# Second edge network: bias added by VectorE while it empties the bank, norm applied by ScalarE cell by cell

## The chip, the cores and the metric

One core of one Trainium2 chip. The metric is the device time of one execution in microseconds, the median of the runs shown; lower is better.

## The reference

Four graph layers in a row over 12500 nodes and 412500 edges. The change lies in the third, a mesh network whose edge state `e` (64 wide) goes through one network per step `s`, two steps:

```python
def _mlp(x, w0, b0, w1, b1):
    return jax.nn.silu(x @ w0 + b0) @ w1 + b1
def _ln(x, g, b):
    m = jnp.mean(x, axis=-1, keepdims=True)
    v = jnp.var(x, axis=-1, keepdims=True)
    return (x - m) * jax.lax.rsqrt(v + LN_EPS) * g + b
...
for s in range(S):
    ce = jnp.concatenate([e, n[senders], n[receivers]], axis=-1)
    e = e + _ln(_mlp(ce, edge_blk_w0[s], edge_blk_b0[s], edge_blk_w1[s], edge_blk_b1[s]), edge_blk_g[s], edge_blk_beta[s])
    agg = jax.ops.segment_sum(e.astype(jnp.float32), receivers, num_segments=num_nodes)
```

"Second edge network" is this line with s = 1. What the change touches is the output `... @ w1 + b1` and the factor `rsqrt(v + eps)` of its layer norm. The mean is taken out of the weights and of the bias ahead of time.

## The kernel before

The edges are sorted by target once and cut into 104 blocks. A block is 128 lanes by 35 cells (tile columns); a cell is 64 numbers on each lane. `sorted_mlp` (L1828) builds a pass over the blocks; it is called for both edge networks, with `rnd` 0 (`enc` true, which also encodes the edges) and `rnd` 1, which is the one in question. The names in the trace are the same for both; they are told apart by time. `PARTS5` (L1822) splits the 35 cells into five groups of 8, 8, 8, 8 and 3 cells, so 512 columns or 192; the last group's matmuls are padded to 256.

For a group of block k of the second network, in order:

- VectorE `picks` (L2079, L2080): three one-hot tables and one of the targets; `windows` (L2145 to L2151) splits the block's window of node rows into three bf16 parts, once a block.
- TensorE `gather` (L2474, L2481, L2486) takes the node terms into a bank `ps_h1`, `hidden1` (L2503) adds the edge state that SP loaded (`states`), with the spilled row (L2496) in the last group.
- ScalarE `act1_` (L2336): silu into `act1`.
- TensorE `out1` (L2506): a matmul of one row of biases into the bank (L2511, `row_eblk`), then eight of the weights (L2514), into one of two banks `ps_o1`.
- ScalarE `out1_` (L2338): copies the bank to `unit1` (L2344), then squares `unit1` into `sq1` (L2348).
- VectorE `var1` (L2139) sums the squares of each cell into `stat`; after all five groups `roots` (L2190 and `newton`, L555 to L569) turns these into scales, once a block.
- VectorE `norm1` (L2094) multiplies a group of `unit1` by its scales.
- The result is split into three bf16 parts for the sum by target: ScalarE `part0` (L2362), VectorE `less0` (L2107), ScalarE `part1` (L2366), VectorE `part2` (L2111). TensorE `part_sums` (L2526, L2528, L2530) adds them up in `ps_sum`, and VectorE `merge` (L2168 to L2180) finishes the block.

Every engine has its order written out by hand, three blocks deep: at turn k TensorE, ScalarE and VectorE work on block k-1 in the network (`main`) and on block k-2 behind the root (`out_`), VectorE also makes the first two groups' picks of block k and merges block k-3. `in_pairs` (L88) writes out six turns and then loops over pairs. There is one `unit1`, so a group of it can be filled only when `less0` of that group of the block before has read it.

VectorE's turn before the change (`body`, L2207; M is block k-1, O is k-2, N is k):

```
for s in 0..4:  picks(M, s+2) if s < 3;  norm1(O, s);  merge(k-3) at s=0;  shifts(O) at s=1
                picks(N, 0), windows(N) at s=4;  less0(O, s-1) from s=1;  part2(O, s-2) from s=2;  var1(M, 0) at s=4
then:           var1(M, 1), less0(O, 4), part2(O, 3), part2(O, 4), picks(N, 1), var1(M, 2..4), roots
```

ScalarE's turn (`body`, L2368) over s = 0..7 is `part0(O, s-1)`, `part1(O, s-2)`, `act1_(M, s-1)`, `out1_(M, s-2)`; TensorE's is `gather(M, s)`, `hidden1(M, s-1)`, `part_sums(O, s-3)`, `out1(M, s-2)`. SP loads rows, tables and states in one queue (`load`, `load_late`, `load_states`, `load_rows`, `load_more_rows`), POOL the spilled rows.

The first network (`body_enc`, L2252) already has its bias added by VectorE (`leave1`, L2122, line L2128) and squares with `square1_` (L2350, line L2355).

Of the kernel before, what the change touches and what calls it, by code (L numbers as in the profile page):

```python
# [111 lines left out]
def _gnn(nc, ctx, ins, out):  # L112
# [110 lines left out]
    lane_out = sb("lane_out", [LANES, 2, D])  # L223
# [10 lines left out]
    with ExitStack() as st:  # L234
# [10 lines left out]
        lane_mean = sb("lane_mean", [LANES, 2], F32, st)  # L245
# [53 lines left out]
        def _(sp):  # L299
# [44 lines left out]
            for n, b in enumerate((ins["L2_gnn_edge_enc_b1"], ins["L2_gnn_edge_blk_b1"][0])):  # L344
                load(lane_out[:, n, :], b.unsqueeze(0).broadcast_to([LANES, D]))
# [97 lines left out]
        def _(dve):  # L443
# [59 lines left out]
            for part in range(2):  # L503
                dve.tensor_scalar(lane_out[:, part, :], lane_out[:, part, :], lane_mean[:, part:part + 1], None, ALU.add).then_inc(split, 1)
            dve.wait_ge(split, n + 4)
# [1322 lines left out]
    def sorted_mlp(st, name, rnd):  # L1828
# [28 lines left out]
        aO = Chain(shared("mlp_out1_s"), again * 5 * BLOCKS, [f"{w}{g}" for g in G_ALL for w in (("square",) if enc else ("copy", "square"))])  # L1857
# [8 lines left out]
        vw = chain(shared("mlp_unit1_v"), [f"{g}" for g in G_ALL])  # L1866
        v0 = chain(shared("mlp_var0_or_part2_v"), LEFT)
        v1 = Chain(shared("mlp_var1_v"), again * len(LEFT) * BLOCKS, LEFT if enc else [f"var{g}" for g in G_ALL])
# [179 lines left out]
        def vector(dve):  # L2048
# [158 lines left out]
            def body(k, x, before):  # L2207
                y = 1 - x
                new, main, out_ = enc and inside(k), mains(k, before), outs(k, before)
                for s in G_ALL:  # L2210
                    if not enc and main and s < NG - 2:
                        picks(k - 1, y, s + 2, before - 1)
                    if main and enc:
                        norm0(k - 1, y, s)
                    if enc and main and 1 <= s < NG - 1:
                        picks(k - 1, y, s + 1, before - 1)
# [4 lines left out]
                    if out_ and s == (3 if enc else 1):  # L2221
# [4 lines left out]
                    if not enc and out_ and s >= 1:  # L2226
                        less0(k - 2, x, s - 1, before - 2)
                    if not enc and out_ and s >= 2:
                        part2(k - 2, x, s - 2)
                    if new and s >= 2:  # L2230
                        var0(k, x, s - 2)
                    if main and s == 4:
                        var1(k - 1, y, 0)
                if new:
                    var0(k, x, 3)
                if main:
                    var1(k - 1, y, 1)
                if not enc and out_:
                    less0(k - 2, x, 4, before - 2)
                    part2(k - 2, x, 3)  # L2240
                if not enc and out_:
# [41 lines left out]
            in_pairs(dve, BLOCKS, 3, body_enc if enc else body)  # L2283

        def scalar(act):
# [52 lines left out]
            def out1_(k, x, s, before):  # L2338
                c, e = PARTS5[s]
                p = (x + s) % 2  # L2340
                act.wait_ge(tO.sem, tO.at(f"{s}", k))
                if before:
                    act.wait_ge(z1.sem, z1.at(f"{s}", k - 1))
                act.activation(unit1[:, c:e, :].rearrange("p c f -> p (c f)"), ps_o1[p % NB][:, 0:width(s)], ACT.Copy).then_inc(aO.sem, 1)  # L2344
                if s >= 2 or before:
# [1360 lines left out]
```

## Time and profile before

| | us |
|---|---|
| median of 3 runs | 16682.69 (16665.74 to 16684.43) |
| profiled execution | 16624.54 |
| its span | 16622.9 |
| busy in the span: TensorE | 13631.4 (82%) |
| VectorE | 12780.7 (77%) |
| ScalarE | 7955.2 (48%) |
| GpSimd | 4541.5 (27%) |
| mean granted TensorE clock | 0.845 of full |

The profile is of one execution, so its rows add up to 16622.9 us and not to the median. The shares are means over some fifteen passes with different limits; the second edge pass lies between about 11740 and 14573 us of the span. An instruction's duration runs to its end; engines start the next one a little before that, so a row's duration is somewhat longer than the distance between two starts.

### The profile page before, as it was taken

How to read it: one execution, taken by the hardware profiler on the slowest of the kernel's cores; microseconds unless marked ns; L12 is line 12 of the kernel's file. 1: busy time of each engine (PE TensorE's matmuls, PEld its weight loads, DVE VectorE, ACT ScalarE, POOL GpSimd, SP SyncE). 2: the span in 40 equal slices, each digit the busy share in tenths (PEclk: the TensorE clock that was granted, in tenths of full speed). 3: DMA queues.
4: the chain of work that ended last, by engine and by line, in shares of the span. 5: the costliest groups of instructions: out<-in, count | busy, mean ns of one | idle time of the engine just before them, and what ended most of it. 6: DMA issues, size and time to landing. Idle time of an engine off the chain costs nothing. (4 is left out here: it accounts for less than half of the span.)

```text
span 16622.9 us, 505597 instructions
## 1 busy us (share of the span) xinstructions
PE 13631.4 (82%) x180600; PEld 11953.3 (72%) x180600; DVE 12780.7 (77%) x30492; ACT 7955.2 (48%) x15316; POOL 4541.5 (27%) x4403
## 2 busy tenths in 40 slices
PE   1677777777767998799999999997799999956665
PEld 0666767667655998688888888886677777746565
DVE  2888888888866998666666666665788888769898
ACT  0455555555542333344454444443344444437675
POOL 0777777777750110011111111110000000001111
PEclk9666666666656998899999999998999999977676
DMA  2122222222223553455545555452444444437575
GB/s 64 54 64 64 64 63 62 63 64 64 64 52 92 156 158 111 106 127 127 127 124 127 126 126 127 126 126 78 147 158 155 157 159 156 151 88 233 183 232 179
DMA packets 1347374, 1955.72 MB, mean 118 GB/s; under 512 B 705453, under 2 KB 923252, under 8 KB 1306316
## 3 DMA queue, kind: packets, MB, share of 16 engines
q1 hardware_dynamic: 1046674, 1621.50, 30.7%
q0 software_dynamic: 209664, 186.01, 7.8%
q10 hardware_dynamic: 90300, 137.10, 2.2%
q8 instruction: 621, 10.17, 0.2%
q14 instruction: 115, 0.94, 0.0%
HBM read 1443.57 MB, written 501.97 MB: 117 GB/s over the span
## 5 line engine op out<-in xcount | busy, mean ns | idle before, releaser
L815 POOL DMA_INDIRECT records<-e_sort_rec,e_sort_index x3224 | 3216.7, 998 | 1034.4 <-issue 954.9
L2481 PEld LDWEIGHTS e_s_ps_h<-e_s_pick,e_s_parts 128*64 128x64 bf16 x61776 | 1899.8, 110 | 175.7 <-issue 6.7
L2481 PE MATMUL e_s_ps_h<-e_s_pick,e_s_parts 128*64 128x128 bf16 x61776 | 1953.9, 219 | 5.4 <-issue 5.4
L2600 POOL DMA_DIRECT2D states<-e_s_second_t x520 | 479.8, 923 | 3916.4 <-ACT e_s_second_t L2329 3847.8
L1212 PEld LDWEIGHTS e_sort_acc<-e_sort_thirds,e_sort_hot 128*128 128x128 f32 x6864 | 1446.2, 327 | 6.3 <-DVE e_sort_hot L995 6.2
L1212 PE MATMUL e_sort_acc<-e_sort_thirds,e_sort_hot 128*128 128x48 f32 x6864 | 1446.0, 406 | 5.6 <-DVE e_sort_hot L995 5.6
L1079 ACT ACTIVATE e_sort_turned<-e_sort_turn 128x512 f32<-128x512 f32 x832 | 485.9, 584 | 1947.0 <-PE e_sort_turn L1175 1947.0
L2079 DVE TENSOR_SCALAR e_s_pick<-e_s_rows,lane_below 128x1024 bf16<-128x1024 bf16 (+1 forms) x3120 | 1177.9, 433 | 223.8 <-PE e_s_ps_h L2481 201.2
L2119 DVE TENSOR_TENSOR e_s_unit<-e_s_ps_o,lane_out 128x512 f32<-128x512 f32 (+1 forms) x520 | 324.7, 625 | 1325.0 <-PE e_s_ps_o L2439 1324.7
L1192 PE MATMUL e_sort_y<-e_sort_window,e_sort_turned 128*128 128x128 f32 x6448 | 1233.0, 351 | 2.5 <-DVE e_sort_prod L952 2.3
L2591 POOL DMA_INDIRECT e_s_spill<-send,e_s_lists x208 | 217.8, 1047 | 3408.4 <-PE e_s_ps_h L2503 2691.5
L1114 ACT ACTIVATE e_sort_away<-iota,e_sort_slots 128x128 f32<-128x128 f32 x3640 | 1105.5, 388 | 6.8
L1192 PEld LDWEIGHTS e_sort_y<-e_sort_window,e_sort_turned 128*128 128x128 f32 x6448 | 1104.0, 257 | 3.3 <-DVE e_sort_prod L952 3.2
L2514 PE MATMUL e_s_ps_o<-w_eblk,e_s_act 128*128 128x128 f32 x7488 | 1013.0, 276 | 0.9 <-DVE e_s_unit L2128 0.9
L2514 PEld LDWEIGHTS e_s_ps_o<-w_eblk,e_s_act 128*128 128x128 f32 x7488 | 949.7, 192 | 47.6 <-issue 35.1
L2302 ACT ACTIVATE e_s_act<-e_s_ps_h,col_eenc 128x512 f32<-128x512 f32 (+1 forms) x520 | 335.1, 644 | 1334.3 <-PE e_s_ps_h L2430 1334.3
L2336 ACT ACTIVATE e_s_act<-e_s_ps_h,col_state 128x512 f32<-128x512 f32 (+1 forms) x1040 | 663.2, 638 | 509.4 <-PE e_s_ps_h L2500 256.7
L2541 PE MATMUL e_s_ps_sum<-e_s_unit,e_s_wide 128*128 128x128 f32 x7280 | 900.0, 276 | 0.1
L2474 PE MATMUL e_s_ps_h<-e_s_to_hot,e_s_window 128*64 128x512 bf16 (+2 forms) x6240 | 804.8, 361 | 96.4 <-DVE e_s_window L2151 82.5
L1175 PE MATMUL e_sort_turn<-ident,e_sort_hot_d 128*128 128x128 bf16 x3224 | 402.3, 261 | 565.2 <-DVE e_sort_hot_d L883 558.1
L2541 PEld LDWEIGHTS e_s_ps_sum<-e_s_unit,e_s_wide 128*128 128x128 f32 x7280 | 855.8, 192 | 0.7 <-issue 0.7
L1783 PE MATMUL e_s_psp<-e_s_wide,e_s_product 128*128 128x128 f32 x7280 | 840.6, 277 | 3.9 <-DVE e_s_product L1683 3.5
(562 smaller groups left out, 32075.7 us busy)
## 6 DMA issues: line engine op xcount, KB each, us to landing
e_s_rows<-rows_d SPq DMA_DIRECT2D x312, 1088.0 KB, 5.4
e_s_hot<-hots_d SPq DMA_DIRECT2D x520, 560.0 KB, 3.9
e_s_to_rows<-rows_d SPq DMA_DIRECT2D x208, 608.0 KB, 5.8
e_s_rows<-rows_d SPq DMA_DIRECT2D x208, 544.0 KB, 4.3
e_s_rows<-rows_d SPq DMA_DIRECT2D x208, 512.0 KB, 5.4
e_s_to_rows<-rows_d SPq DMA_DIRECT2D x208, 512.0 KB, 6.2
states<-e_s_first_t ACTq DMA_DIRECT2D x416, 256.0 KB, 2.1
states<-e_s_second_t POOLq DMA_DIRECT2D x416, 256.0 KB
```

What stands on the lines that cost most here:

```text
L815: pool.indirect_dma_start(records, bass.IndirectOffsetOnAxis(ap=index[x][:, t:t + 1], axis=0), rec[x][:, t, :], None,).then_inc(written[x] ...
L1079: act.activation(turned[x][:, t:e, :].rearrange("p t q -> p (t q)"), ps_turn[:, 0:(e - t) * LANES], ACT.Copy).then_inc(as_.sem, 1)
L1114: last = act.activation(away[:, n - c, :], iota128[:, :], ACT.Square, scale=-1.0, bias=slots[x][:, n, 1:2])
L1192: mm = pe.matmul(ps_y[j % 2][0:LANES, (n - t) * AF:(n - t + 1) * AF], turned[x][:, n, :], window[x][:, :], start=True, stop=True)
L1212: mm = pe.matmul(acc[sum_bank(c)][:, sum_at(c)], hot[:, c, :], thirds[:, c, :, :].rearrange("p h f -> p (h f)"), start=False, stop=last an ...
L1783: mm = pe.matmul(ps_spread[:, 0:LANES], product[x][:, c].rearrange("p a f -> p (a f)"), wide[:, c * LANES:(c + 1) * LANES], start=c == 0, ...
L2079: dve.tensor_scalar(pick[p][:, h, 0:(f - c) * LANES], rows_[:, c * LANES:f * LANES], lane_below[:, h:h + 1], None, ALU.is_equal).then_inc( ...
L2336: act.activation(act1[p][:, 0:turned(s)], hidden_bank(x, s)[:, 0:turned(s)], ACT.Silu, bias=(col_state if enc else col_state1)[:, :]).then ...
L2474: pe.matmul(halves[half][:, 0:n_ * LANES], window[:, r, 1, :], to_pairs[:, half, 0:n_, :], start=r == 0, stop=False, skip_group_check=True)
L2481: mm = pe.matmul(halves[half][:, j * LANES:(j + 1) * LANES], parts[:, SPAN * c + h, r, :], pick[p][:, h, (c - c0) * LANES:(c - c0 + 1) * L ...
L2514: mm = pe.matmul(ps_o1[p % NB][:, j * LANES:(j + 1) * LANES], act1[p][:, j * LANES:(j + 1) * LANES], W[f"eblk1{rnd}"][:, :], start=enc, st ...
L2541: mm = pe.matmul(ps_sum[:, 0:2 * D if enc else D], wide[s][:, (c - c0) * LANES:(c - c0 + 1) * LANES], units_of(x, c), start=c == 0, stop=F ...
```

## The change

VectorE's copy of the biases, `lane_out`, gets a third plane for the second network's output bias, centred like the others. In that network `out1` leaves out the bias matmul (L2511). `out1_` is gone: VectorE empties the bank with `leave1`, adding the bias, and ScalarE only squares (`square1_`). `norm1` is not called there: ScalarE's new `scaled1` multiplies each cell of `unit1` in place by its column of `stat`, one activation a cell, 35 a block, and signals `vw` after each group. VectorE's turn is written anew as `body_blk`; ScalarE's has `scaled1(O, s)` first at each s and the square at s-3. The first network's order stays.

```diff
-    lane_out = sb("lane_out", [LANES, 2, D])
+    lane_out = sb("lane_out", [LANES, 3, D])
...
-            for n, b in enumerate((ins["L2_gnn_edge_enc_b1"], ins["L2_gnn_edge_blk_b1"][0])):
+            for n, b in enumerate((ins["L2_gnn_edge_enc_b1"], ins["L2_gnn_edge_blk_b1"][0], ins["L2_gnn_edge_blk_b1"][1])):
                 load(lane_out[:, n, :], b.unsqueeze(0).broadcast_to([LANES, D]))
...
-            for part in range(2):
+            for part in range(3):
                 dve.tensor_scalar(lane_out[:, part, :], lane_out[:, part, :], lane_mean[:, part:part + 1], None, ALU.add).then_inc(split, 1)
...
             def leave1(k, x, s, before):
                 c, e = PARTS5[s]
                 dve.wait_ge(tO.sem, tO.at(f"{s}", k))
-                if before:
+                if before and enc:
                     dve.wait_ge(ts.sem, ts.at(f"{s}", k - 1))
                     dve.wait_ge(tw.sem, tw.at(f"{s}", k - 1))
+                if before and not enc:
+                    dve.wait_ge(z1.sem, z1.at(f"{s}", k - 1))
                 dve.tensor_tensor(unit1[:, c:e, :], ps_o1[(x + s) % 2 % NB][:, 0:width(s)].rearrange("p (c f) -> p c f", f=D),
-                                  lane_out[:, 1:2, :].broadcast_to([LANES, e - c, D]), ALU.add).then_inc(v1.sem, 1)
+                                  lane_out[:, 1 + rnd:2 + rnd, :].broadcast_to([LANES, e - c, D]), ALU.add).then_inc(v1.sem, 1)
...
+            def body_blk(k, x, before):
                 y = 1 - x
+                main, out_ = mains(k, before), outs(k, before)
                 for s in G_ALL:
+                    if main and s < NG - 2:
                         picks(k - 1, y, s + 2, before - 1)
-                    if out_:
-                        norm1(k - 2, x, s)
                     if before >= 3 and s == 0:
                         merge(k - 3, y, before - 3)
+                    if out_ and s == 1:
                         shifts(k - 2, x, before - 2)
                     if inside(k) and s == NG - 1:
                         picks(k, x, 0, before)
                         windows(k, x, before)
+                    if out_ and s >= 1:
                         less0(k - 2, x, s - 1, before - 2)
+                    if out_ and s >= 2:
                         part2(k - 2, x, s - 2)
+                    if main and s >= 3:
+                        leave1(k - 1, y, s - 3, before - 1)
+                    if main and s >= 4:
+                        var1(k - 1, y, s - 4)
+                if out_:
                     less0(k - 2, x, 4, before - 2)
                     part2(k - 2, x, 3)
+                if main:
+                    leave1(k - 1, y, 2, before - 1)
+                    var1(k - 1, y, 1)
+                if out_:
                     part2(k - 2, x, 4)
                 if inside(k):
                     picks(k, x, 1, before)
                 if main:
+                    leave1(k - 1, y, 3, before - 1)
                     var1(k - 1, y, 2)
+                    leave1(k - 1, y, 4, before - 1)
                     var1(k - 1, y, 3)
                     var1(k - 1, y, 4)
                 if inside(k) or main:
                     roots(k, before)
...
+            def scaled1(k, x, s):
+                c, e = PARTS5[s]
+                if s == 0:
+                    act.wait_ge(vr.sem, vr.end(k + 1))
+                act.wait_ge(aO.sem, aO.at(f"square{s}", k))
+                for n in range(c, e):
+                    mm = act.activation(unit1[:, n, :], unit1[:, n, :], ACT.Copy, scale=stat[:, 0, CELLS + n:CELLS + n + 1])
+                mm.then_inc(vw.sem, 1)
...
+                    if not enc and out_ and s < NG:
+                        scaled1(k - 2, x, s)
                     if not enc and out_ and 1 <= s < NG + 1:
                         part0(k - 2, x, s - 1, before - 2)
...
                     if not enc and main and 1 <= s < NG + 1:
                         act1_(k - 1, y, s - 1, before - 1)
-                    if not enc and main and 2 <= s < NG + 2:
-                        out1_(k - 1, y, s - 2, before - 1)
+                    if main and s >= 3:
+                        square1_(k - 1, y, s - 3, before - 1)
...
                 if s >= NB or before:
-                    pe.wait_ge((v1 if enc else aO).sem, group_at(v1, "leave", k, s, NB) if enc else group_at(aO, "copy", k, s, NB))
-                if not enc:
-                    pe.matmul(ps_o1[p % NB][:, 0:turned(s)], ones3[:, :], row3[f"eblk1_{rnd}"][:, 0:turned(s)], start=True, stop=False)
+                    pe.wait_ge(v1.sem, group_at(v1, "leave", k, s, NB))
                 pe.wait_ge(aH.sem, aH.at(f"{s}", k))
```

## Rows read from the trace of the kernel before

**Rows 1.** The merge in the second pass: ns min/median/max, first and last start.

```profile
L2168 DVE TENSOR_REDUCE e_s_scaled<-e_s_ps_sum x104: 343/350/357, 11767.1 to 14572.5; 128x64 f32<-128x192 f32 x104
```

**Rows 2.** Busy us by engine, granted clock, DMA share, GB/s over 400 us.

```profile
12800.00:13200.00 400.00, 384.66 (x6281) 300.41 (x6280) 324.87 (x873) 192.18 (x364) 14.63 (x14) 1.00 0.49 159
```

**Rows 3.** Timeline of TensorE around one block: start, us, merged instructions.

```profile
13019.54 0.43 PE L2530 MATMUL e_s_ps_sum<-e_s_split,e_s_hot 128*128 128x193 bf16 x3
...
13026.14 1.12 PE L2503 MATMUL e_s_ps_h<-e_s_states,w_eblk_e 128*128 128x512 f32 x2 [0.73 <-DMA e_s_states<-states]
...
13029.97 1.13 PE L2503 MATMUL e_s_ps_h<-e_s_states,w_eblk_e 128*128 128x512 f32 x2
...
13030.93 0.38 PE L2511 MATMUL e_s_ps_o<-row_eblk,ones 128*128 128x512 bf16 x1
...
13031.15 1.05 PE L2514 MATMUL e_s_ps_o<-w_eblk,e_s_act 128*128 128x128 f32 x8
...
13046.96 0.17 PE L2528 MATMUL e_s_ps_sum<-e_s_zeros 1*128 1x1 bf16 x1 [0.56 <-DVE e_s_split L2111]
```

**Rows 4.** Timeline, VectorE and ScalarE in the same block.

```profile
13022.45 0.18 DVE L2190 TENSOR_SCALAR e_s_stat<-e_s_stat 128x35 f32<-128x35 f32 x1
...
13024.28 0.20 DVE L569 SCALAR_TENSOR_TENSOR e_s_stat<-e_s_stat 128x35 f32<-128x35 f32 x1
13024.39 1.27 DVE L2079 TENSOR_SCALAR e_s_pick<-e_s_rows,lane_below 128x1024 bf16<-128x1024 bf16 x3
...
13025.98 0.68 DVE L2094 TENSOR_TENSOR e_s_unit<-e_s_unit,e_s_stat 128x512 f32<-128x512 f32 x1
...
13031.92 0.68 DVE L2107 TENSOR_TENSOR e_s_less<-e_s_unit,e_s_split 128x512 f32<-128x512 f32 x1
...
13038.99 0.23 DVE L2145 CAST e_s_window<-e_s_window_in 128x128 bf16<-128x128 f32 x1 [1.71 <-PE e_s_ps_h L2486]
...
13040.05 0.69 DVE L2107 TENSOR_TENSOR e_s_less<-e_s_unit,e_s_split 128x512 f32<-128x512 f32 x1
...
13040.65 0.68 DVE L2111 TENSOR_TENSOR e_s_split<-e_s_less,e_s_split 128x512 bf16<-128x512 f32 x1
...
13043.18 0.35 ACT L2362 ACTIVATE e_s_split<-e_s_unit 128x192 bf16<-128x192 f32 x1
...
13043.65 0.36 DVE L2107 TENSOR_TENSOR e_s_less<-e_s_unit,e_s_split 128x192 f32<-128x192 f32 x1 [1.12 <-ACT e_s_split L2362]
...
13046.16 0.35 ACT L2366 ACTIVATE e_s_split<-e_s_less 128x192 bf16<-128x192 f32 x1
...
13046.54 0.36 DVE L2111 TENSOR_TENSOR e_s_split<-e_s_less,e_s_split 128x192 bf16<-128x192 f32 x1 [1.77 <-ACT e_s_split L2366]
```

**Rows 5.** ScalarE by form in the pass: busy us, mean ns | idle before.

```profile
L2336 ACT ACTIVATE e_s_act<-e_s_ps_h,col_state 128x512 f32<-128x512 f32 x416 | 280.7, 675 | 248.1 <-PE e_s_ps_h L2503 247.8
...
L2348 ACT ACTIVATE e_s_sq<-e_s_unit 128x512 f32<-128x512 f32 x416 | 262.0, 630 | 14.4
L2362 ACT ACTIVATE e_s_split<-e_s_unit 128x512 bf16<-128x512 f32 x416 | 258.7, 622 | 723.7 <-DVE e_s_unit L2094 723.7
...
L2344 ACT ACTIVATE e_s_unit<-e_s_ps_o 128x512 f32<-128x512 f32 x416 | 247.9, 596 | 318.4 <-PE e_s_ps_o L2514 317.1
...
L2348 ACT ACTIVATE e_s_sq<-e_s_unit 128x192 f32<-128x192 f32 x104 | 37.7, 363 | 248.0 <-DVE e_s_stat L2139 247.9
```

**Rows 6.** Timeline of the first edge network: its addition, and the square behind it.

```profile
8018.89 0.69 DVE L2128 TENSOR_TENSOR e_s_unit<-e_s_ps_o,lane_out 128x512 f32<-128x512 f32 x1 [0.38 <-PE e_s_ps_o L2514]
...
8019.62 0.63 ACT L2355 ACTIVATE e_s_sq<-e_s_unit 128x512 f32<-128x512 f32 x1
```

**Rows 7.** ScalarE by line and form over the whole span.

```profile
L1114 ACT ACTIVATE e_sort_away<-iota,e_sort_slots 128x128 f32<-128x128 f32 x3640 | 1105.5, 388 | 6.8
...
L2329 ACT ACTIVATE e_s_second_t<-e_s_ps_w,gain_col 128x512 f32<-128x512 f32 x416 | 281.9, 678 | 11.7 <-PE e_s_ps_w L2458 10.0 <-DMA states<-e_s_second_t 1.6
```

**Rows 8.** Timeline of ScalarE in the sort: nine activations in a row.

```profile
2010.87 2.74 ACT L1114 ACTIVATE e_sort_away<-iota,e_sort_slots 128x128 f32<-128x128 f32 x9
```

More of the change, by code:

```diff
@@ L244, in _gnn @@
         lane_more = sb("lane_more", [LANES, D], F32, st)
-        lane_mean = sb("lane_mean", [LANES, 2], F32, st)
+        lane_mean = sb("lane_mean", [LANES, 3], F32, st)
         parts = {k: sb(f"parts_{k}", [1, 2, S * D], F32, st) for k in row3}
@@ L502, in _ @@
             dve.wait_ge(split, n + 2)
-            for part in range(2):
+            for part in range(3):
                 dve.tensor_scalar(lane_out[:, part, :], lane_out[:, part, :], lane_mean[:, part:part + 1], None, ALU.add).then_inc(split, 1)
-            dve.wait_ge(split, n + 4)
+            dve.wait_ge(split, n + 5)
             dve.tensor_reduce(span[:, 0:1], span_t[:, :], axis=AX.X, op=ALU.max).then_inc(ordered, 1)
@@ L1856, in sorted_mlp @@
         aH = chain(shared("mlp_act1_s"), [f"{g}" for g in G_ALL])
-        aO = Chain(shared("mlp_out1_s"), again * 5 * BLOCKS, [f"{w}{g}" for g in G_ALL for w in (("square",) if enc else ("copy", "square"))])
+        aO = Chain(shared("mlp_out1_s"), again * 5 * BLOCKS, [f"square{g}" for g in G_ALL])
         aw = chain(shared("mlp_second_or_part1_s"), [f"{g}" for g in G_ALL])
@@ L1865, in sorted_mlp @@
         vu = chain(shared("mlp_unit0_or_less_v"), [f"{g}" for g in G_ALL])
-        vw = chain(shared("mlp_unit1_v"), [f"{g}" for g in G_ALL])
+        vw = chain(shared("mlp_unit1"), [f"{g}" for g in G_ALL])
         v0 = chain(shared("mlp_var0_or_part2_v"), LEFT)
-        v1 = Chain(shared("mlp_var1_v"), again * len(LEFT) * BLOCKS, LEFT if enc else [f"var{g}" for g in G_ALL])
+        v1 = Chain(shared("mlp_var1_v"), again * len(LEFT) * BLOCKS, LEFT)
         vr = Chain(shared("mlp_rsqrt_v"), again * RSQRT_STEPS * (BLOCKS + 1), rsqrt_names("dev"))
@@ L2281, in body_enc @@
                     both_roots(k, before)
-            in_pairs(dve, BLOCKS, 3, body_enc if enc else body)
+            in_pairs(dve, BLOCKS, 3, body_enc if enc else body_blk)
         def scalar(act):
@@ L2336, in act1_ @@
                 act.activation(act1[p][:, 0:turned(s)], hidden_bank(x, s)[:, 0:turned(s)], ACT.Silu, bias=(col_state if enc else col_state1)[:, :]).then_inc(aH.sem, 1)
[L2338 to L2345, printed above, removed]
-                    act.wait_ge(v1.sem, group_at(v1, "var", k, s, 2))
-                act.wait_ge(aO.sem, aO.at(f"copy{s}", k))
-                act.activation(sq1[p][:, 0:width(s)], unit1[:, c:e, :].rearrange("p c f -> p (c f)"), ACT.Square).then_inc(aO.sem, 1)
             def square1_(k, x, s, before):
@@ L2396, in body @@
                         square0_(k, x, s - 2, before)
-                    if enc and main and s >= 3:
-                        square1_(k - 1, y, s - 3, before - 1)
                     if not enc and main and 1 <= s < NG + 1:
                         act1_(k - 1, y, s - 1, before - 1)
-                    if not enc and main and 2 <= s < NG + 2:
-                        out1_(k - 1, y, s - 2, before - 1)
+                    if main and s >= 3:
+                        square1_(k - 1, y, s - 3, before - 1)
             in_pairs(act, BLOCKS, 2, body)
@@ L2514, in out1 @@
                     mm = pe.matmul(ps_o1[p % NB][:, j * LANES:(j + 1) * LANES], act1[p][:, j * LANES:(j + 1) * LANES], W[f"eblk1{rnd}"][:, :],
-                                   start=enc, stop=enc or j == pairs(s)[-1])
+                                   start=True, stop=True)
                 mm.then_inc(tO.sem, 1)
```

20 lines of the change are left out of this document (removed).

## The prediction

> **What bounds the kernel now.** Only the second edge network changes, so I first looked for its stretch and the length of one block. Its merge instruction runs once a block, 104 times, the first at 11767.1 us and the last at 14572.5 us [rows 1]: 2805.4 / 103 = 27.24 us a block. The pass is about 2833 us of the 16622.9 us span; all else is untouched. Then the busy time of its engines: in 400 us TensorE 384.66, VectorE 324.87, ScalarE 192.18, at full granted clock [rows 2]. In 27.24 us that is 26.2, 22.1 and 13.1 us. Third, the order of time on TensorE: its matmuls follow each other without a break except, above all, for a wait for the loaded states (0.73 us) and one for VectorE's last split (0.56) [rows 3]. VectorE has three longer gaps, of 1.71, 1.12 and 1.77 us [rows 4]: the first waits for TensorE, the others for ScalarE, which itself keeps waiting for TensorE's output. So TensorE sets the pace, VectorE is some 5 us behind it, ScalarE has half of its time free.
>
> **What the change removes.** TensorE loses the bias matmul ahead of each group. It starts at 13030.93 and the next matmul at 13031.15 [rows 3]: 0.22 us for a full group, about half for the last: 4 x 0.22 + 0.11 = 0.99 us a block. If nothing else moved, a block would take 26.25 us. ScalarE loses five copies out of the matmul's bank, 0.596 us for each full group [rows 5]. VectorE loses five multiplies of 0.68 us [rows 4] and gains five additions of 0.69 us [rows 6], to be read in the first network, where the same addition exists: nothing in sum (0.01 us each).
>
> **What it adds.** ScalarE gets 35 activations a block, each of 64 columns with a column of scales. No row has just that; I bound it from two sides. The nearest row is L1114, the sort's activation with a column as bias, 128 columns, 0.388 us alone [rows 7]; nine in a row take 2.74 us [rows 8], so (2.74 - 0.388) / 8 = 0.294 us from start to start, an overlap of 0.094. The slope is (0.630 - 0.363) / 320 = 0.83 ns a column [rows 5], so 64 columns fewer take off 0.053: 0.241 us. The other way: 0.363 for 192 columns, less 128 x 0.83 = 0.107, plus what a scale column adds (0.678 with it [rows 7] against 0.596 without [rows 5], 0.082), less the overlap: 0.244. I take 0.24, so 1.92 us for a group of eight; the upper bound is 0.335 without overlap.
>
> The Trainium skill (ScalarE: Activation LUTs, What ACT_TABLE_LOAD costs) gives 93 ns for each pointer operand where the rows' difference is 82, and 0.239 us for the whole; by it the sum below would be about 0.03 us a block less, by 0.244 it would be 0.13 more. The rows decide, and the two differ by less than I can tell.
>
> ScalarE's work is then 13.1 - 2.7 + 8.4 = 18.8 us a block: it doesn't become the bound by its load. The question is where the 8.4 us lie. The scaling begins only when VectorE's root has ended, and each of ScalarE's and VectorE's following steps hangs on the other in turn (scale, part0, less0, part1, part2).
>
> **The chain, step by step.** M is the block in the network, O the one before it, whose norm is applied, N the next. A step is counted from start to start, in full where somebody waits for its end. Durations: part0 and part1 0.53 (0.62 in full), activation of the hidden layer 0.58, square 0.54 [rows 5] (less 0.09 overlap); on VectorE 0.60 for 512 columns, 0.28 for 192, a group's picks 1.59, the window 1.06, the root 2.03 [rows 4]; the addition 0.61, in full 0.69 [rows 6]. Handing over costs 0.12 us from ScalarE to less0 (13043.18 + 0.35 to 13043.65) and 0.04 to part2 (13046.16 + 0.35 to 13046.54) [rows 4]; addition to square 0.04 (8018.89 + 0.69 to 8019.62) [rows 6]. From the root to ScalarE no row shows it; I take 0.12, the larger of the two, since there too two waits stand ahead.
>
> From the root's end (0): ScalarE waits 0.12 and scales groups 0 and 1, 3.96; part0 of group 0, 4.49; hidden activation 0 of M, 5.07; scales group 2, 6.99; part0 of 1 and part1 of 0, 8.05; hidden activation 1, 8.63; scales group 3, 10.55; part0 of 2 ends 11.17. VectorE gets there sooner: before, less0 of group 1 began at 13031.92, 7.53 us after the first pick and behind three multiplies [rows 4], so it now stands and waits, 2.3 us in its longest gap. At 11.29 it runs less0 of 2, part2 of 1 (12.49), the addition of M's group 0 (13.10), N's first picks (14.69), the window (15.75), less0 of 3, part2 of 2 (16.95), the addition of group 1, in full (17.64). Queued behind each of VectorE's new waits are N's picks or M's variances, and for them wait TensorE's next gathers and the root. Now ScalarE again: square of 1 from 17.68, part0 of 4 (18.48), part1 of 3, in full (19.10). VectorE: part2 of 3 (19.74), addition of 2, in full (20.43). ScalarE: square of 2 (21.01), part1 of 4, in full (21.36). VectorE: part2 of 4 (21.68), N's second picks (23.27), addition of 3, variance of 2, addition of 4, variances of 3 and 4 (25.71), the root 25.74 to 27.77. So a block takes **27.8 us**, 0.53 more than now, by a chain without TensorE in it.
>
> **Does TensorE fit under it?** Its 25.2 us of work do. The last part2 ends near 21.75; its sums end at 22.35 and the next two gathers at 28.0. The SP queue sends the hot table ahead of the states; from the last sums' start to the first hidden matmul went 6.6 us (13019.54 to 13026.14), and with that it starts at 28.4, 0.65 after the root. A hidden matmul and a gather take 3.8 us (13026.14 to 13029.97), a hidden and a group of outputs now 2.0, a gather 2.8 [rows 3]: gather 2 ends at 4.5, outputs 0 at 6.5, gather 3 at 9.3, hidden 2 at 10.4. ScalarE asks for hidden 0 at 4.5 (there 1.7), and for hidden 2 at 11.6, the tightest place, with 1 us to spare; the outputs are ready well before the additions. I judge TensorE off the path. SP and POOL send what they did; SP's loads of rows hang on the picks as before. Setup gains one DMA and one VectorE addition of 64 columns, under 1 us.
>
> The sum: 104 x 0.53 = +55 us. The profiled execution took 16624.54 us, 58 below the runs' median of 16682.69; the difference is put on the median: **16738 us**, +0.33%. Handovers are the soft part: some ten of them, 0.04 us off each is 0.4 us a block. So this case spans 27.4 to 28.3 us a block, +17 to +110 us. A run can tell about 0.2% (33 us) from no change.
>
> **Rivals.** *TensorE stays the bound* (chance 0.14): its work falls to 25.2 us, its 1.0 us of waits stays, and a block takes 26.25: 104 x 0.99 = -103, 16580 us. Its place is ScalarE's start after the root; it decides if the chain is under 26.25, so 1.5 us shorter than mine. For it speaks that TensorE was the pace-setter and is relieved [rows 2, 3]; against it that 32 x 0.24 = 7.7 us of scaling stand in series ahead of less0 of group 2, where VectorE's multiplies took 0.60 a group.
> *Even* (0.21): the handovers come out cheap, or one of them is hidden, and the chain ends within 0.3 us of the old pace: 26.95 to 27.55 us a block, 16650 to 16715 us.
> *The small activations don't overlap* (0.05): 32 x 0.095 = 3.0 us more on the chain, 104 x 3.5 = +368, 17050 us. Rows 8 speak against it, though there the output and input are different tiles, and here it is in place.
> *TensorE's clock falls* (0.06): its idle share goes from 4% to some 9%. The clock granted in the pass is 1.00, so 2.4 GHz [rows 2]; a quarter of its time at 1.2 GHz would make its 25.2 us 25.2 / 0.875 = 28.8, with 1.0 of waits 29.8, 104 x 2.6 = +270, 16950 us. For it speaks that the waits grow in one place (the states, over 0.7 us); against it that in the rows nothing falls at such waits. The Trainium skill (TensorE: Matmul & The Clock Gate, Part 1) has the clock halved when the engine idles; by it this rival would come true only where the waits are long, and no run here shows what these do.
> My forecast has the rest, 0.54. The slower side holds 0.54 + 0.05 + 0.06 = 0.65. The range leaves out the faster rival's centre and the two dear ones: 16630 to 16850.
>
> **What would show it.** Right: in the pass L2168's spacing is 27.4 to 28.3 us; the scaling's start-to-start is 0.24 us; ScalarE's wait for VectorE's L569 stands where its waits for L2094 were; VectorE waits over 2 us for part0 and no longer 1.7 us for TensorE's gather; TensorE is busy 91 to 93%, with its clock at 1.00. Wrong: a spacing of 26.3 with TensorE near 96% and no long wait of VectorE for part0; or the scaling at 0.33 us each; or a granted clock under 0.95.

## The result, and the profile after

| | kernel before | changed kernel |
|---|---|---|
| median, us | 16670.36 (20 runs, 16657.74 to 16685.03) | 16712.06 (20 runs, 16692.06 to 16737.97) |
| ratio, 95% interval | | 1.0024 [1.0018, 1.0031] |
| profiled span, us | 16622.9 | 16717.7 |
| merge to merge in the second pass, us | 27.24 | 27.56 |
| TensorE, VectorE, ScalarE busy in 400 us | 384.15, 322.13, 193.60 | 369.13, 319.26, 269.58 |

The change costs 0.24%, +30 to +52 us on 16670. (Busy times are means over 12000 to 14400 us.) The two profiled spans differ by 95 us, but some 60 us of that are there before the second edge network starts, where of the change only the set-up's one load and one small addition run: the first edge network's table split begins at 6725.2 us in the one and at 6789.0 in the other, and the second pass's first merge is 60.7 us later. What made these 60 us is not known; the profiled execution of the kernel before is also 46 us under its median. So the pass is to be compared by itself, and its spacing is the measure in all that follows.

The merge of the changed kernel, all 104 of them, answers to [rows 1]:

```profile
L2170 DVE TENSOR_REDUCE e_s_scaled<-e_s_ps_sum x104: 345/349/357, 11827.8 to 14666.3; 128x64 f32<-128x192 f32 x104
```

2838.5 / 103 = 27.56 us, 0.32 more than before; the whole stretch of merges grew by 33.1 us. The busy times of a stretch of 400 us (x is the number of instructions; then the granted clock, the DMA share and GB/s) answer to [rows 2]:

```profile
12800.00:13200.00 400.00, 370.16 (x6055) 287.92 (x6049) 318.06 (x850) 272.59 (x802) 13.24 (x14) 1.00 0.48 155
```

TensorE has fallen from 96% to 92.5%, at the same clock of 1.00, while the block grew: something else sets the pace now. Next, ScalarE by line and form over the pass (count, busy us, mean ns, idle time before it and its releaser), against [rows 5]:

```profile
L2348 ACT ACTIVATE e_s_unit<-e_s_unit,e_s_stat 128x64 f32<-128x64 f32 x3640 | 910.2, 335 | 284.5 <-DVE e_s_stat L569 284.5
L2333 ACT ACTIVATE e_s_act<-e_s_ps_h,col_state 128x512 f32<-128x512 f32 x416 | 278.8, 670 | 104.8 <-PE e_s_ps_h L2497 104.8
L2340 ACT ACTIVATE e_s_sq<-e_s_unit 128x512 f32<-128x512 f32 x416 | 262.3, 631 | 618.4 <-DVE e_s_unit L2130 618.2
```

The first line is the new scaling: 3640 small activations, 335 ns each alone. Its wait is for L569, the root's last step, as the prediction said it would be. The reader should see the last line too: the squares wait 618 us for VectorE's additions, where before those of the full groups waited next to nothing for anybody (14.4 us, [rows 5]), the copies ahead of them having waited for TensorE. TensorE has left ScalarE's waits: the 104.8 us in the second line all belong to the pass's start (91.1 us of them are the wait for its first hidden layer). From 12000 to 14400 us the same line reads

```profile
L2333 ACT ACTIVATE e_s_act<-e_s_ps_h,col_state 128x512 f32<-128x512 f32 x347 | 232.4, 670 | 0.0
```

where the kernel before waited 119.6 us for TensorE in that stretch.

The list of waits of the changed kernel, 12000 to 14400 us, 87 blocks (us in total, times, longest), says who waits now:

```profile
ACT e_s_sq L2340 <- DVE e_s_unit L2130: 544.9, 435, 2.6
DVE e_s_less L2107 <- ACT e_s_split L2356: 372.4, 304, 2.2
ACT e_s_unit L2348 <- DVE e_s_stat L569: 236.6, 86, 2.8
...
PE e_s_ps_sum L2520 <- DVE e_s_split L2111: 103.3, 174, 0.9
...
DVE e_s_split L2111 <- ACT e_s_split L2360: 30.9, 87, 0.4
```

ScalarE waits for VectorE and VectorE for ScalarE, in turn, and TensorE waits for both; VectorE's wait of 1.71 us for TensorE's gather [rows 4] is gone. The timeline of one block of the changed kernel shows the loop itself (start, us, instruction, idle time before it). It answers to [rows 3, 4]:

```profile
13017.35 0.20 DVE L569 SCALAR_TENSOR_TENSOR e_s_stat<-e_s_stat 128x35 f32<-128x35 f32 x1
...
13017.68 3.93 ACT L2348 ACTIVATE e_s_unit<-e_s_unit,e_s_stat 128x64 f32<-128x64 f32 x16 [2.80 <-DVE e_s_stat L569]
...
13018.13 1.13 PE L2497 MATMUL e_s_ps_h<-e_s_states,w_eblk_e 128*128 128x512 f32 x2 [0.33 <-DMA e_s_states<-states]
...
13021.51 0.61 ACT L2356 ACTIVATE e_s_split<-e_s_unit 128x512 bf16<-128x512 f32 x1
...
13028.77 0.69 DVE L2107 TENSOR_TENSOR e_s_less<-e_s_unit,e_s_split 128x512 f32<-128x512 f32 x1 [2.23 <-ACT e_s_split L2356]
...
13034.42 0.68 DVE L2130 TENSOR_TENSOR e_s_unit<-e_s_ps_o,lane_out 128x512 f32<-128x512 f32 x1
...
13035.13 0.63 ACT L2340 ACTIVATE e_s_sq<-e_s_unit 128x512 f32<-128x512 f32 x1 [1.48 <-DVE e_s_unit L2130]
...
13037.18 0.68 DVE L2130 TENSOR_TENSOR e_s_unit<-e_s_ps_o,lane_out 128x512 f32<-128x512 f32 x1
...
13037.32 0.17 PE L2520 MATMUL e_s_ps_sum<-e_s_zeros 1*128 1x1 bf16 x1 [0.52 <-DVE e_s_split L2111]
...
13038.43 0.35 ACT L2360 ACTIVATE e_s_split<-e_s_less 128x192 bf16<-128x192 f32 x1
...
13038.81 0.36 DVE L2111 TENSOR_TENSOR e_s_split<-e_s_less,e_s_split 128x192 bf16<-128x192 f32 x1 [0.36 <-ACT e_s_split L2360]
...
13043.27 0.18 DVE L2192 TENSOR_SCALAR e_s_stat<-e_s_stat 128x35 f32<-128x35 f32 x1 [0.20 <-DVE e_s_stat L2141]
...
13045.09 0.20 DVE L569 SCALAR_TENSOR_TENSOR e_s_stat<-e_s_stat 128x35 f32<-128x35 f32 x1
...
13045.32 0.82 ACT L2348 ACTIVATE e_s_unit<-e_s_unit,e_s_stat 128x64 f32<-128x64 f32 x3 [2.71 <-DVE e_s_stat L569]
```

Counted from the root's end at 13017.55 the forecast chain can be checked link by link:

| link, us after the root's end | forecast | measured |
|---|---|---|
| ScalarE starts scaling | 0.12 | 0.13 (0.03 one block later, 13045.29 to 13045.32) |
| groups 0 and 1 scaled, part0 of 0 starts | 3.96 | 3.96 |
| less0 of group 2 starts | 11.29 | 11.22 |
| addition 1 ends | 17.64 | 17.55 |
| square of group 1 starts | 17.68 | 17.58 |
| addition 2 ends | 20.43 | 20.31 |
| part2 of group 4 starts | 21.40 | 21.26 |
| root starts | 25.74 | 25.72 |
| root ends | 27.77 | 27.74 |

The last links agree by two errors that cancel. By the last part2 the chain is 0.14 us ahead of the forecast, in hundredths along the additions; then the root waits 0.20 us for the last variance (the line at 13043.27; 17.2 us in 87 blocks), where the forecast had put 0.03. TensorE's part came out as judged: its first hidden matmul starts 0.58 us after the root (forecast 0.65). At the tightest place, hidden activation 2, it is ready 0.6 us early in this block instead of 1 us, since it had waited 0.56 us for the hot table's lanes.

### The profile page after: what moved, and what is told of

Read it like the earlier page. It is cut to its first block and busy times, and to the rows that moved or that the text cites. A ratio compares the mean times of both kernels' runs of the same rounds, so it can differ in the third digit from the quotient of the medians.

```text
span 16717.7 us, 507070 instructions
## 1 busy us (share of the span) xinstructions
PE 13575.6 (81%) x180080; PEld 11900.6 (71%) x180080; DVE 12793.9 (77%) x30493; ACT 8520.8 (51%) x18436; POOL 4591.5 (27%) x4403
## 5 line engine op out<-in xcount | busy, mean ns | idle before, releaser
L815 POOL DMA_INDIRECT records<-e_sort_rec,e_sort_index x3224 | 3259.7, 1011 | 1034.3 <-issue 958.6
L2348 ACT ACTIVATE e_s_unit<-e_s_unit,e_s_stat 128x64 f32<-128x64 f32 x3640 | 910.2, 335 | 284.5 <-DVE e_s_stat L569 284.5
L2340 ACT ACTIVATE e_s_sq<-e_s_unit 128x512 f32<-128x512 f32 (+1 forms) x1040 | 598.5, 575 | 727.6 <-DVE e_s_unit L2130 727.5
```

What stands on the lines that cost most here:

```text
L815: pool.indirect_dma_start(records, bass.IndirectOffsetOnAxis(ap=index[x][:, t:t + 1], axis=0), rec[x][:, t, :], None,).then_inc(written[x] ...
L2340: act.activation(sq1[(x + s) % 2][:, 0:width(s)], unit1[:, c:e, :].rearrange("p c f -> p (c f)"), ACT.Square).then_inc(aO.sem, 1)
L2348: mm = act.activation(unit1[:, n, :], unit1[:, n, :], ACT.Copy, scale=stat[:, 0, CELLS + n:CELLS + n + 1])
```

## The experiments

All ratios are to the kernel before, measured in turn on the same chip, with their 95% intervals. "Spacing" is merge to merge over the whole pass. Theory A is the prediction's: a loop between VectorE and ScalarE sets the pace of the changed kernel, with the scaling in it. Its rivals: the load of ScalarE as such, TensorE with its loads, VectorE's new order, or one small cost in the change.

### The two halves apart: e1, e2, and the matmul put back, e3

e1 keeps the addition at the evacuation and gives the norm back to VectorE:

```diff
                     if main and s < NG - 2:
                         picks(k - 1, y, s + 2, before - 1)
+                    if out_:
+                        norm1(k - 2, x, s)
...
-                    if not enc and out_ and s < NG:
-                        scaled1(k - 2, x, s)
```

e2 is the kernel before (bias matmul, ScalarE's copies) with `scaled1` on ScalarE in place of `norm1` on VectorE. e3 is the changed kernel with the bias matmul issued again; the matmul that follows overwrites it:

```diff
                     pe.wait_ge(v1.sem, group_at(v1, "leave", k, s, NB))
+                if not enc:
+                    pe.matmul(ps_o1[p % NB][:, 0:turned(s)], ones3[:, :], row3[f"eblk1_{rnd}"][:, 0:turned(s)], start=True, stop=True)
                 pe.wait_ge(aH.sem, aH.at(f"{s}", k))
```

> The changed kernel with its norm back on VectorE (norm1 where it stood in the old order) and no scaling on ScalarE: the bias half of the change alone. Chain theory (the 32 scalings in series ahead of less0 of group 2 set the block): they are gone, less0 of 2 starts some 9.4 us after the root instead of 11.2, VectorE has 25.1 us of work, TensorE 25.2 plus its waits, so 26.3 to 26.6 us a block, 65 to 100 us under the kernel before. Rival (VectorE empties the bank from within its long queue, TensorE's outputs wait for it, and that is the loss): 27.5 us a block or more, 30 us or more over the kernel before.

> The kernel before with only its norm moved to ScalarE, one activation a cell; bias matmul and ScalarE's copy stay. Chain theory: by the same steps the chain is 26.1 us here, since no addition and no late square lies on it, so it stays under TensorE's 27.2: 27.2 to 27.6 us a block, 0 to 40 us over the kernel before. Rival (ScalarE's load of small activations is the cost, whatever the order): ScalarE has more work here than in the changed kernel, 21.5 against 18.8 us, so slower than that, over +60 us.

> The changed kernel, with the bias matmul still issued into the bank and then overwritten: TensorE gets its 0.99 us a block back, nothing else differs. Chain theory: TensorE has some 2 us of slack, so 0 to 15 us over the changed kernel, +40 to +60 over the kernel before. Rival (TensorE is still the pace): 0.99 us a block, 103 us over the changed kernel, about +145.

| | ratio | spacing | TensorE, VectorE, ScalarE busy in 400 us |
|---|---|---|---|
| e1 bias half alone | 0.9939 [0.9926, 0.9952] | 26.19 | 385.96, 374.05, 164.99 |
| e2 scaling half alone | 1.0003 [0.9994, 1.0012] | 27.30 | 382.34, 284.69, 309.38 |
| e3 change, matmul kept | 1.0021 [1.0012, 1.0030] | 27.59 | 378.44, 319.79, 269.21 |

The bias half alone gains 0.61%, some 100 us (80 to 123 by the interval), at or over the upper end of what was expected, and its 26.19 us are under the expected 26.3. It keeps VectorE's new order, so that order isn't the loss. The scaling half alone is even, though ScalarE works more there (309 us in 400) than in the changed kernel (270). So ScalarE's load is not what costs; the changed kernel loses because both halves are in it, where each alone loses nothing. In e2 VectorE waits for part0 in 481.9 us of 2400 (105.1 before), so the scaling does lengthen that path; but ScalarE's copies still wait for TensorE, 71.3 us in all (267.7 before), while the changed kernel's ScalarE waits for TensorE nowhere in that stretch. That the loop of e2 is just shorter than TensorE's pace, 26.1 us by the expectation's count, fits this and was not tested by itself.

And e3 shows that TensorE has room in the changed kernel: its busy time grew by 9.3 us in 400, and the spacing by only 0.03 us, where the rival needs 0.99. The growth is a lower bound: 520 weight loads of the bias matmul stand in e3's trace and only 209 of the matmuls themselves, so three in five have no record (e2's trace lacks as many; those of the kernel before and of e8 are whole). The ratio, +20 to +50 us, reaches the lower part of the +40 to +60 expected. This refutes the rival that TensorE stays the bound.

The merges of e1 and of e2:

```profile
L2170 DVE TENSOR_REDUCE e_s_scaled<-e_s_ps_sum x104: 346/352/358, 11807.9 to 14505.3; 128x64 f32<-128x192 f32 x104
```

```profile
L2168 DVE TENSOR_REDUCE e_s_scaled<-e_s_ps_sum x104: 348/351/358, 11784.6 to 14596.6; 128x64 f32<-128x192 f32 x104
```

### Is the scaling's place or its amount what costs? e5 and e6

Both add the same eight activations of 64 columns with a scale column to each block of the changed kernel, into a scratch tile. e5 puts two at the head of each of groups 0 to 3; e6 puts all eight after the last square, where ScalarE waits 2.7 to 2.8 us for the root.

```diff
                 act.wait_ge(aO.sem, aO.at(f"square{s}", k))
+                for n in range(c, c + 2 if s < NG - 1 else c):
+                    act.activation(scratch[:, 2 * s + n - c, :], ident128[:, 0:D], ACT.Copy, scale=lane[:, 0:1])
                 for n in range(c, e):
```

> The changed kernel with two more activations of 64 columns, into a tile nobody reads, at the head of the scaling of each of groups 0 to 3: eight of 0.24 us, all ahead of less0 of group 2. Chain theory: 1.92 us a block more, 29.5 us, 200 us over the changed kernel, +230 to +250 over the kernel before. Rival (ScalarE has 9 us a block free, the loss is elsewhere): +40 as the changed kernel.

> The same eight activations, put behind the last square of ScalarE's turn, where it waits 2.7 us for the root. Chain theory: hidden, 0 to 15 us over the changed kernel, so +35 to +55 over the kernel before, 27.6 us a block. Rival (ScalarE's sum of work, or its number of instructions, is what costs): as the run with eight on the chain, +230.

The merges of e5, then of e6:

```profile
L2171 DVE TENSOR_REDUCE e_s_scaled<-e_s_ps_sum x104: 344/351/358, 11838.3 to 14870.4; 128x64 f32<-128x192 f32 x104
```

```profile
L2171 DVE TENSOR_REDUCE e_s_scaled<-e_s_ps_sum x104: 346/350/357, 11811.7 to 14649.2; 128x64 f32<-128x192 f32 x104
```

e5: 1.0145 [1.0129, 1.0160], 29.44 us a block, 1.88 more than the changed kernel: 8 x 0.235, all of it paid. e6: 1.0013 [1.0004, 1.0022], 27.55 us a block: nothing paid. Its time, +7 to +37 us, lies mostly under the +35 to +55 expected and under the changed kernel's own +30 to +52, though the intervals overlap; the spacing is the changed kernel's to 0.01 us. The timeline of ScalarE in e6 shows where they went:

```profile
13024.71 0.36 ACT L2341 ACTIVATE e_s_sq<-e_s_unit 128x192 f32<-128x192 f32 x1 [0.23 <-DVE e_s_unit L2131]
13024.98 2.00 ACT L2400 ACTIVATE e_s_scratch<-ident,lane 128x64 f32<-128x64 f32 x8
13027.78 3.93 ACT L2349 ACTIVATE e_s_unit<-e_s_unit,e_s_stat 128x64 f32<-128x64 f32 x16 [0.80 <-DVE e_s_stat L569]
```

The wait for the root shrank from 2.8 to 0.80 us, and the scaling starts 0.03 us after the root, as in every other block of the changed kernel. This is the strongest evidence for theory A: the same work costs 1.88 us a block in one place and nothing in another.

### What does the scale column cost? e7

e7 scales by a constant, so that only the operand differs: `scale=0.5` in place of `scale=stat[...]`. The norm's factor is left out of its result.

> The changed kernel with the constant 0.5 as the scale in place of the column, so the norm's factor is left out of the result; as many activations of as many columns. It prices the column: start to start 0.15 us instead of 0.24. Chain theory: the chain is 32 x 0.09 = 2.9 us shorter, 24.7, and TensorE sets the pace with 25.2 plus its waits: 26.2 to 26.5 us a block, 80 to 105 us under the kernel before. Rival (what costs is the count of small instructions): no change against the changed kernel, +40.

The scaling of e7 by form over the pass (count, busy us, mean ns, idle before):

```profile
L2348 ACT ACTIVATE e_s_unit<-e_s_unit 128x64 f32<-128x64 f32 x3640 | 573.3, 242 | 284.7 <-DVE e_s_stat L569 284.7
```

242 ns against 335: the column costs 93 ns an activation, and it isn't hidden: sixteen in a row take 2.45 us instead of 3.93, 0.147 from start to start instead of 0.240. The prediction had read 0.082 for it from rows of 512 columns. The Trainium skill (ScalarE: Activation LUTs, What ACT_TABLE_LOAD costs) gives a fixed cost, a slope by columns and 93 ns for a pointer operand; an estimate from its figures for 64 columns is 332 ns with the column and 239 without. The traces agree within 3 ns (335 and 242).

The kernel then runs at 0.9951 [0.9936, 0.9966] and 26.35 us a block, with TensorE at 384.45 of 400 again: once 32 x 0.093 = 3.0 us leave the loop, something else sets the pace, and only 1.2 of the 3.0 show. By its busy share that is TensorE with its waits.

### Less of the norm on ScalarE: e4 and e9

e4 gives groups 0 and 2 back to VectorE, as its multiply of 0.60 us each; ScalarE scales 1, 3 and 4.

> The changed kernel, with groups 0 and 2 multiplied by VectorE (0.60 us each, in gaps where it waited) and groups 1, 3, 4 scaled by ScalarE. Chain theory: less0 of group 2 starts some 10.1 us after the root instead of 11.2, the chain is 26.4 us, about TensorE's own pace: 26.3 to 26.7 us a block, 60 to 100 us under the kernel before. Rival (the loss is in the bank's emptying, not in the scaling): unchanged, +30 to +50.

e4: 0.9981 [0.9972, 0.9990], 26.93 us a block: faster than the changed kernel by 0.63 us a block, but about half of the 0.9 to 1.3 that was expected. Its timeline (start, us, idle before) shows what was overlooked:

```profile
13031.64 2.02 ACT L2355 ACTIVATE e_s_unit<-e_s_unit,e_s_stat 128x64 f32<-128x64 f32 x8 [2.74 <-DVE e_s_stat L569]
...
13034.65 0.61 ACT L2363 ACTIVATE e_s_split<-e_s_unit 128x512 bf16<-128x512 f32 x1
...
13036.81 0.68 DVE L2096 TENSOR_TENSOR e_s_unit<-e_s_unit,e_s_stat 128x512 f32<-128x512 f32 x1
...
13037.60 0.69 DVE L2109 TENSOR_TENSOR e_s_less<-e_s_unit,e_s_split 128x512 f32<-128x512 f32 x1
...
13038.32 0.63 ACT L2367 ACTIVATE e_s_split<-e_s_less 128x512 bf16<-128x512 f32 x1 [3.06 <-DVE e_s_less L2109]
...
13042.08 0.69 DVE L2109 TENSOR_TENSOR e_s_less<-e_s_unit,e_s_split 128x512 f32<-128x512 f32 x1 [1.87 <-ACT e_s_split L2363]
```

VectorE reaches less0 of group 0 only at 13037.60, behind the picks of its program order; ScalarE's next instruction, part1 of group 0, waits 3.06 us for it, and the scaling of group 3 queues behind that. Two groups of scaling, 3.9 us, were taken off ScalarE, and it spent most of them in this wait: less0 of group 2 starts 10.57 us after the root's end (13031.51) instead of 11.22. These 0.65 us are what the block became shorter by (0.63): the chain still sets the pace.

e9 puts the split where that can't happen: VectorE multiplies groups 0 to 2 as in the kernel before, ScalarE scales groups 3 and 4 in the time in which it waits for VectorE anyway.

```diff
                         picks(k - 1, y, s + 2, before - 1)
+                    if out_ and s in MINE:
+                        norm1(k - 2, x, s)
...
-                    if not enc and out_ and s < NG:
-                        scaled1(k - 2, x, s)
+                    if not enc and out_ and s == 0:
+                        scaled1(k - 2, x, 3)
+                        scaled1(k - 2, x, 4)
```

`MINE` is the groups 0, 1 and 2.

> The changed kernel, with groups 0 to 2 multiplied by VectorE where the old order had them, and ScalarE scaling only groups 3 and 4, both at once when the root ends, 2.7 us in which it had nothing to do. Chain theory: no step of VectorE waits for these 11 activations, VectorE has 24.2 us of work against 25.1 in the bias half alone; TensorE's 25.2 plus its wait for the states set the pace: 25.9 to 26.2 us a block, 105 to 140 us under the kernel before. Rival (scaling on ScalarE costs wherever it stands, by its work): slower than the bias half alone, 26.5 us or more.

e9: 0.9947 [0.9934, 0.9961], 26.28 us a block: 65 to 111 us under the kernel before, where 105 to 140 were expected, and 0.08 us a block above the expected range. The scaling is free in this place: VectorE's busy time is 361 in 400 against e1's 374. But nothing is won over e1 (0.9939 [0.9926, 0.9952]), for VectorE now waits 0.8 us a block for TensorE's gather, as it did before [rows 4].

### Was it the matmul that the bias half saved? e8

e8 is e1 with the overwritten bias matmul of e3.

> The bias half alone (norm on VectorE, bias added by VectorE), with the bias matmul still issued and overwritten. If the gain of the bias half is TensorE's 0.99 us a block, it is gone: 27.1 to 27.3 us a block, within 20 us of the kernel before. If it comes from ScalarE's five copies or from the new order, it stays: 26.2 us and 95 us under the kernel before.

e8: 0.9968 [0.9957, 0.9979], 26.72 us a block: between the two answers that were expected. Of e1's gain of 1.05 us a block, 0.53 goes when the matmul comes back and 0.52 stays. TensorE's busy time a block is 26.1 us in e8 (390.62 x 26.72 / 400) and 26.2 in the kernel before, so the 0.52 are not work: its idle time fell from 1.08 to 0.63 us a block. The waits of TensorE, 12000 to 14400 us, say what; in the kernel before (us in total, times, longest)

```profile
PE e_s_ps_sum L2528 <- DVE e_s_split L2111: 48.9, 88, 0.6
PE e_s_ps_h L2503 <- DMA e_s_states<-states: 33.5, 68, 1.1
PE e_s_ps_h L2474 <- DVE e_s_pick L2079: 12.2, 44, 0.3
```

and in e8

```profile
PE e_s_ps_h L2497 <- DMA e_s_states<-states: 41.9, 81, 1.0
PE e_s_ps_h L2468 <- DVE e_s_to_hot L2080: 11.9, 30, 0.8
```

The wait for part2 (0.56 us a block) is gone; that for the states grew a little. Before, ScalarE's part0 and part1 stood in its queue behind copies which themselves waited for TensorE's outputs (317.1 us in the pass, [rows 5]); the addition took those copies out of that queue. So the likely reason is that the bias half breaks a loop that ran through TensorE; that the wait goes is shown, that it goes for this reason is argued from the rows, and no run separates the missing copies from VectorE's new order, which e8 also has. The prediction had put 1.0 us of TensorE's waits down as staying.

### The order of the loads: e10, e11, e12

TensorE's other wait in the kernel before is for the states. These runs move SP's loads of the first two states ahead of the hot table:

```diff
+                if states_in_use:
+                    load_states(k - 1, 1 - x, before - 1, (0, 1))
                 if mains(k, before):
                     load_late(k - 1, 1 - x, before - 1)
-                if states_in_use:
-                    load_states(k - 1, 1 - x, before - 1, (0, 1))
```

in e9's kernel (e10), in the changed kernel (e11) and in the kernel before (e12).

> As the run before, and SP sends the states of groups 0 and 1 ahead of the hot table, so that they don't wait for the end of the last sums. If TensorE is the pace and its 0.7 to 0.9 us a block of waiting for the states is on its path: 25.3 to 25.7 us a block, 150 to 200 us under the kernel before. If VectorE's queue is the pace by now: no gain over the run before.

> The changed kernel with only that order of SP's loads. Chain theory: TensorE is off the path, its wait for the states is slack: within 15 us of the changed kernel, +25 to +50 over the kernel before, 27.5 us a block. Rival (TensorE on the path): 0.5 us a block less, 50 us under the changed kernel.

> The kernel before with only that order of SP's loads. If TensorE paced it, its wait of 0.73 us for the states goes: 26.5 to 26.8 us a block, 45 to 75 us under the kernel before. If the pace is the loop through ScalarE's copies and VectorE, it is unchanged.

| | ratio | spacing | without the new order |
|---|---|---|---|
| e10, on e9 | 0.9939 [0.9926, 0.9953] | 26.24 | 26.28 |
| e11, on the changed kernel | 1.0018 [1.0009, 1.0027] | 27.55 | 27.56 |
| e12, on the kernel before | 0.9975 [0.9966, 0.9985] | 26.79 | 27.24 |

The one edit is worth 0.45 us a block in the kernel before and nothing in the changed kernel: the two kernels have different bounds, and TensorE is on the path of the first (e12's 25 to 57 us are at or under the low end of the 45 to 75 expected). On e9 it was expected to give 0.6 us or more and gave 0.04. The waits of TensorE in e10 name what came in its place:

```profile
PE e_s_ps_h L2473 <- DVE e_s_to_hot L2082: 69.1, 91, 0.9
PE e_s_ps_h L2473 <- DVE e_s_pick L2081: 11.9, 46, 0.3
```

The wait for states is gone, and TensorE waits 0.76 us a block for the hot table's lanes from VectorE instead (0.27 in e1).

## Why the prediction held, and where its sum was off

**The direction and the mechanism.** Forecast: a chain from the root through the scaling, the splits, the additions and the squares, without TensorE, of 27.8 us. Shown: the table of links above, each within 0.14 us; e5 and e6, which price the same work on and off the chain; e3 and e11, which show that TensorE and its loads are off it. The signs it named are all there: 27.56 us of spacing (27.4 to 28.3 forecast), 0.240 us from start to start (0.24), the wait for L569, over 2 us of VectorE for part0, TensorE at 92.3% (91 to 93), the clock at 1.00. The measured +42 us of medians (16712.06 - 16670.36) lies in its range of +17 to +110 for that case, with the centre, +55, a little high. The time itself, 16712, is 26 us under the forecast 16738: 13 of them are the sum, and 12 are the kernel before, whose median over 20 runs is that much under the three runs that the forecast started from.

How well a number came out says less than the links do: 16712 lies also inside the 16650 to 16715 of the rival *even*, so by the time alone the two can't be told apart. It is the chain, checked link by link and moved by e4 and e5, that decides for the forecast's mechanism.

**The size.** The forecast was +55 us; the pass shows +33 and the runs +30 to +52. Two terms of equal size are to blame. The first is the step "2805.4 / 103 = 27.24 us a block", which the chain's 27.77 was measured against. The start of the root in the kernel before and in the changed one, 12000 to 14400 us (ns min/median/max, first and last start):

```profile
L2190 DVE TENSOR_SCALAR e_s_stat<-e_s_stat x88: 181/182/184, 12012.8 to 14391.6; 128x35 f32<-128x35 f32 x88
```

```profile
L2192 DVE TENSOR_SCALAR e_s_stat<-e_s_stat x87: 181/182/184, 12018.9 to 14399.7; 128x35 f32<-128x35 f32 x87
```

In the steady part a block took 2378.8 / 87 = 27.34 us before and takes 2380.8 / 86 = 27.68 now. The merges' mean is lower because the last merge comes only 11.0 us after the one before it (16.8 in the changed kernel), when no new block runs beside it. A chain counted within one steady block should have been held against 27.34: 0.10 us too much, 10 us in 104 blocks. The second is the chain's own length, 27.77 against 27.68: 9 us. About half of it is the handover from the root to ScalarE, 0.03 us in every other block where 0.12 was put (the two kinds of block take 27.63 and 27.74 us); the rest is what is left of the hundredths gained along the additions after the root's new wait has taken most of them back. 55 - 10 - 9 = 36, with 33 measured in the pass.

**TensorE's relief.** "TensorE loses 0.99 us a block" was too much. With the matmul put back, TensorE's busy time a block grows by 0.82 us in the traces whose records are whole ((390.62 x 26.72 - 385.96 x 26.19) / 400, e8 against e1), and by at least (378.44 x 27.59 - 369.13 x 27.56) / 400 = 0.67 us in e3. The block itself grows by only 0.53 us from e1 to e8, because e1 has 0.29 us more of waits. So the 0.22 us from the start of a bias matmul to the start of the next [rows 3] was somewhat too dear, and part of what leaves TensorE comes back as waiting. This term didn't enter the forecast, but it was the price of the faster rival: 26.25. e1 and e7 reach 26.19 and 26.35 all the same, with the help of something that the rival didn't have, the vanished wait for part2.

**The rivals.** *TensorE stays the bound*: refuted by e3 and e11 for the changed kernel, and near the truth as soon as the loop is shortened (e7, 26.35). *Even*: it had 26.95 to 27.55 us a block; the pass came to 27.56, just outside its edge, and the time inside its range. Half of the way there is the base of 27.24; only the other half is what the rival named, cheaper handovers. *The small activations don't overlap*: refuted, sixteen take 3.93 us, in place as well. *TensorE's clock falls*: 1.00 in all six stretches of 400 us with 7.7% idle.

**What stays open.** e9 and e10 stop at 26.2 to 26.3 us a block like e1, although VectorE is relieved in both and the states come in time in e10. TensorE works 25.2 to 25.3 us of that; the waits name VectorE's picks and lanes for TensorE and TensorE's gather for VectorE, so a loop between these two is likely, but no run took it apart. Also open: the 9 us between the pass's +33 and the medians' +42; they are inside the interval. And no run shows why the root waits 0.20 us for its last variance in the changed kernel.

## What to carry to other kernels

Before moving work to the engine with the most free time, trace the loop of in-order queues that it joins: 7.7 us in series after the root cost nothing while the rest of the loop was short (e2), and turned a gain of some 100 us into a loss of 40 when the other half of the change put its own steps into the same loop. When a change has two halves, run each alone; and to learn whether an engine's work is on the pacing loop, add a few cheap instructions in two places (e5, e6), since busy shares don't tell. Take a block's length from the steady part of a loop, not over its drain, when a forecast hangs on a few tenths of a microsecond.

## What the runs showed of the hardware

- A scale column costs a 64-column activation 93 ns (335 against 242), and back to back nearly all of it remains: 0.240 us from start to start against 0.147. The overlap between neighbours, 0.095 us, is the same with and without it. The same operand cost 0.082 in the rows of 512 columns [rows 5, 7].
- Work done in place overlaps as well as work between different tiles: 0.095 us here, 0.094 in [rows 8].
- The root reaches the waiting ScalarE in 0.13 us in one block and in 0.03 in the next, by turns: blocks of 27.74 and 27.63 us follow each other for it. What in the two bodies of the unrolled pair makes the difference was not tried.
- TensorE's clock stayed at 1.00 (2.4 GHz) with 7.7% of its time idle in waits of up to 1.0 us, and it stayed there with 12.7% in e5 (349.4 busy of 400), in waits of up to 1.2 us.
- A trace can lack most records of one kind of instruction: in e2 and e3 three in five bias matmuls have none, while their weight loads do, so TensorE's busy time is read too low there.
